# Transpositions in one pass, new orders of the work, and two experts' gates on GpSimd

## The reference, cut to what matters

```
# layer 0: attention, then a mixture of experts with one choice of experts for each image
q, k, v = 1x1 convolutions of LN_c(x)            # 8 query heads of 16, one key and value head
u0 = x + conv_out(softmax(q) @ (softmax(k) v^T))
logits = mean over tokens(LN_t(u0)) @ Wr          # one row of 8 for each image
top 2 of 8 experts: z = sum_w( gelu(u W1[e]) W2[e] )
t = u0 + LN_t(z + u) * gamma                      # u = LN_t(u0)
# layer 1: a 3x3 convolution with weights of sign(w), then experts chosen for each token
t = t + conv3x3(LN_c(t), sign(w) * mean|w|)
xn = LN_t(t);  p = softmax(xn @ gate_w);  g = p where p is one of the token's 2 largest, else 0
out = t + sum over all 8 experts of  g[:, e] * (gelu(xn W1[e]) W2[e])
```

## Time and profile before

| | |
|---|---|
| Median of the runs | 410.23 us (408.69, 410.23, 413.77) |
| The profiled execution's own time | 412.51 us |
| Its span, first to last instruction | 410.7 us |
| Mean granted clock of TensorE | 0.927 |
| TensorE matmuls busy | 344.7 us, 84% of the span |
| VectorE / ScalarE / GpSimd busy | 278.7 / 230.0 / 92.8 us |
| Start of expert 2's hidden matmuls, images 1 to 6 | 205.94, 235.85, 265.74, 295.64, 325.54, 355.44 us |

### The profile page before, as it was taken

One profiled execution on the slowest core, in us unless ns is written; L12 is line 12 of the kernel. 1 busy time (PEld: TensorE's weight loads), 2 busy tenths in 40 slices (PEclk: granted clock), 3 DMA queues, 4 the chain that ended last, 5 costly groups with the idle time before them and its releaser, 6 DMA issues.

```text
span 410.7 us, 5254 instructions
## 1 busy us (share of the span) xinstructions
PE 344.7 (84%) x1751; PEld 188.1 (46%) x1751; DVE 278.7 (68%) x587; ACT 230.0 (56%) x392; POOL 92.8 (23%) x77
## 2 busy tenths in 40 slices
...
GB/s 153 178 119 31 1 2 2 0 2 1 2 1 0 0 2 1 0 74 339 1 103 336 0 128 311 0 155 285 0 207 233 0 229 211 3 292 144 26 344 95
DMA packets 25835, 41.17 MB, mean 100 GB/s; under 512 B 15376, under 2 KB 16144, under 8 KB 25808
## 3 DMA queue, kind: packets, MB, share of 16 engines
...
...
## 4 chain that ended last, share of the span: by engine, by line
PE 41%; DVE 25%; issue 13%; ACT 10%; POOL 5%; DMA 3%; POOLq 1%; ACTq 0%; SPq 0%; DVEq 0%
PE ps L696 9%; PE ps L742 6%; PE ps L801 5%; POOL rstdA L457 4%; PE ps L605 3%; PE ps L712 3%; DVE HB L1186 3%; PE ps L618 2%; PE ps L530 2%; PE ps L513 2%; PE ps L727 2%; DVE qsum L964 2%; ACT XC L1336 2%; ACT HB L1388 2%; DVE ssA L1092 2%
## 5 line engine op out<-in xcount | busy, mean ns | idle before, releaser
L696 PE MATMUL ps<-ET,W1B 64*128 64x512 f32 x256 | 70.4, 655 | 6.9 <-ACT HB L1388 5.3
L1186 DVE TENSOR_TENSOR HB<-HB,GB 128x1024 f32<-128x1024 f32 x44 | 53.1, 1220 | 23.9 <-DMA GB<-spread 23.8
L1388 ACT ACTIVATE HB<-ps,B1B 128x1024 f32<-128x1024 f32 x44 | 47.8, 1111 | 9.4 <-PE ps L696 5.3
L457 POOL TENSOR_TENSOR rstdA<-varA,pow_half 128x8 f32<-128x8 f32 x16 | 28.8, 1801 | 90.8 <-DVE varA L886 90.8
L801 PE MATMUL ps<-HB,W2B 128*64 128x512 f32 x176 | 45.2, 617 | 3.7 <-DVE HB L1186 3.7
L457 POOL TENSOR_TENSOR rstdB<-varB,pow_half 128x8 f32<-128x8 f32 x8 | 14.0, 1750 | 124.7 <-DVE varB L886 124.7
L696 PEld LDWEIGHTS ps<-ET,W1B 64*128 64x128 f32 x256 | 21.9, 194 | 35.8 <-issue 12.0
L457 POOL TENSOR_TENSOR rstd<-var,pow_half 128x4 f32<-128x4 f32 (+1 forms) x24 | 29.0, 1217 | 21.1 <-DVE var L886 20.8
L742 PE MATMUL ps<-VP,WC 128*128 128x512 f32 x96 | 28.4, 450 | 1.4 <-ACT VP L1356 1.4
L1186 DVE TENSOR_TENSOR XC<-XC,GB 128x1024 f32<-128x1024 f32 x20 | 24.2, 1219 | 5.9 <-DMA GB<-spread 5.9
L472 POOL TENSOR_TENSOR QS<-QS,rqsum 128x512 f32<-128x512 f32 x16 | 16.9, 1057 | 44.1 <-DVE rqsum L967 44.1
...
## 6 DMA issues: line engine op xcount, KB each, us to landing
...
```

Of the source, the lines that this page charges most:

```text
L457: pool.tensor_tensor(out_, var, pow_half[:, 0:n], ALU.pow).then_inc(s[rstd_sem], 1)
L696: mm(ps[:, H_BANKS[n % 2][c], :], weights[half(c), :], tokens(half(c)), start=True, stop=True).then_inc(s["h"], 1)
L1186: tt(HG[b][e], HG[b][e], GB[:, e, :], ALU.mult).then_inc(s["f_hg"], 1)
L1388: av(HG[b][e], HID[n % 2], ACT.Gelu, bias=B1B[:, e:e + 1]).then_inc(s["gelu"], 1)
```

## The change

1. `residual` splits its 256-column matmul: the copy of x is now written by TensorE's transposition (`is_transpose=True`), the centred half stays a plain matmul with 128 columns. `u_to_channels` and the residual part of `f_start` become transpositions too.
2. `u_to_channels` no longer has the column of ones. ScalarE's copy into `UT` becomes two instructions with `accum_out`, which give the sums over tokens.
3. `f_start` now holds only the residual, and opens the accumulator before the outputs; the bias is a step of its own, `f_bias`.
4. GpSimd multiplies the hidden values of experts 4 and 7 with their gates, by the same kind of instruction as VectorE; each has its own semaphore, and SyncE's queue and `f_output` wait for the one that belongs to the expert.
5. All tables of orders are new. In the image tables the period begins at another step.

```diff
     return Steps(eng, sem, base)
 
 
+POOL_EXPERTS = (4, 7)
+
+
+def gated(b, e):
+
+    on_pool = e in POOL_EXPERTS
+    mine = [x for x in range(E) if (x in POOL_EXPERTS) == on_pool]
+    return "f_pg" if on_pool else "f_hg", len(mine) * b + mine.index(e) + 1
+
+
...
 PLAN = dict(
     pool=(
-        "b_rstd+1 a_rstd0+2 a_rstd1+2"
+        "f_gated4-1 a_rstd1+1 f_gated7-1 b_rstd+1 a_rstd0+2"
     ).split(),
...
+        "f_hidden6-1 f_hidden7-1 b_to_channels f_bias-1 b_gates f_start f_output2-1 f_hidden0 f_hidden1 "
         "f_output3-1 f_output4-1 f_hidden2 a_hidden0+2 b_gates_turned f_hidden3 f_hidden4 a_vT0+1 f_output5-1 "
...
     vec=(
-        "b_probs b_first a_ss1+1 b_second b_weights a_normalise+1 f_gated5-1 f_gated6-1 f_gated7-1 f_gated0 "
-        "b_residual+1 b_centre+1 f_gated1 b_ss+1 a_sum+2 f_gated2 a_ss0+2 b_normalise+1 f_gated3 a_zn+2 f_gated4 "
-        "b_logits+1 a_residual+2 a_centre+2"
+        "b_normalise f_gated3-1 a_zn+1 a_residual+1 b_logits a_centre+1 b_probs a_ss1+1 b_first b_second b_weights "
+        "a_normalise+1 f_gated5-1 f_gated6-1 f_gated0 f_gated1 b_residual+1 b_centre+1 f_gated2 b_ss+1 a_sum+2 "
+        "a_ss0+2"
...
 )
...
-        "rstd1_0 qnorm2-1 rstd1_1 rstd2_0-1 rstd2_1-1 qnorm3-1 qnorm0 qnorm1 rstd2_2-1 rstd2_3-1"
+        "qnorm3-2 rstd2_1-2 qnorm0-1 rstd2_2-2 qnorm1-1 rstd2_3-2 rstd1_0 rstd1_1 qnorm2-1 rstd2_0-1"
...
-        UT = sb("UT", [P, B, 4, P + 1])
+        UT = sb("UT", [P, B, 4, P])
+        USUM = sb("USUM", [P, B, 4])
...
                 for e in range(E):
-                    ge(sp, s["f_hg"], 8 * (b - 1) + e + 1)
+                    if b > 0:
+                        signal, count = gated(b - 1, e)
+                        sp.wait_ge(s[signal], count)
                     sp.dma_start(GB[:, e, :], spread[b, e:e + 1, :].broadcast_to([P, S])).then_inc(s[f"spread{e}"], 16)
...
+            def f_gated(e):
+                def part(b, par):
+                    pool.wait_ge(s["gelu"], TURN["f", e, b] + 1)
+                    pool.wait_ge(s[f"spread{e}"], 16 * (b + 1))
+                    pool.tensor_tensor(HG[b][e], HG[b][e], GB[:, e, :], ALU.mult).then_inc(s["f_pg"], 1)
+                return part
...
                         pe.wait_ge(s["u"], n - 1)
                     for j in range(UT_):
                         t = g + 4 * j
-                        ins = mm(a[:, j * 256:(j + 1) * 256], XC[:, p, t * P:(t + 1) * P], ic, start=(j == 0), stop=False,
+                        both = a[:, j * 256:(j + 1) * 256].rearrange("p (i x c) -> p i x c", i=2, x=2)
+                        mm(both[:, :, 0, :], XC[:, p, t * P:(t + 1) * P], ident, start=(j == 0), stop=False,
+                           is_transpose=True, skip_group_check=True)
+                        ins = mm(both[:, :, 1, :], XC[:, p, t * P:(t + 1) * P], cen, start=False, stop=False,
                                  skip_group_check=True)
...
                     for i in range(2):
-                        ins = mm(ps[:, UT_BANK, i * (P + 1):(i + 1) * (P + 1)],
-                                 U[:, 2 * p + i, UT_ * g:UT_ * g + UT_, :].rearrange("p h c -> p (h c)"), IDS[:, :],
-                                 start=True, stop=True)
+                        ins = pe.transpose(ps[:, UT_BANK, i * P:(i + 1) * P],
+                                           U[:, 2 * p + i, UT_ * g:UT_ * g + UT_, :].rearrange("p h c -> p (h c)"), ident)
...
             def f_start(b, par):
 
+                pe.wait_ge(s["b_t"], b + 1)
+                ge(pe, s["f_out"], b - 1)
                 for j in range(4):
-                    mm(acc(b)[:, j * P:(j + 1) * P], B2X[:, j, :], GT[:, par, :], start=False, stop=False,
-                       skip_group_check=True)
                     ins = mm(acc(b)[:, j * P:(j + 1) * P], TF[:, par, j].rearrange("p h c -> p (h c)"), ident,
-                             start=False, stop=False, skip_group_check=True)
+                             start=(j == 0), stop=False, is_transpose=True, skip_group_check=True)
                 ins.then_inc(s["f_start"], 1)
+
+            def f_bias(b, par):
+
+                pe.wait_ge(s["b_cwt"], b + 1)
+                for j in range(4):
+                    ins = mm(acc(b)[:, j * P:(j + 1) * P], B2X[:, j, :], GT[:, par, :], start=False, stop=False,
+                             skip_group_check=True)
+                ins.then_inc(s["f_bias"], 1)
...
             def f_output(e):
                 def part(b, par):
-                    if e == 0:
-                        ge(pe, s["f_out"], b - 1)
-                    pe.wait_ge(s["f_hg"], 8 * b + e + 1)
+                    signal, count = gated(b, e)
+                    pe.wait_ge(s[signal], count)
                     for c in range(2):
                         ins = mm(acc(b)[c * C:(c + 1) * C, :], W2B[:, e, :], HG[b][e][:, c * HALF:(c + 1) * HALF],
-                                 start=(e == 0), stop=(e == E - 1), skip_group_check=True)
+                                 start=False, stop=(e == E - 1), skip_group_check=True)
                     ins.then_inc(s["f_w2"], 1)
...
-            rd.done(vr(u8[:, :], UT[:, :, :, P], X, ALU.add))
+            rd.done(vr(u8[:, :], USUM[:, :, :], X, ALU.add))
...
-                [(f"f_gated{e}", f_gated(e)) for e in range(E)]
+                [(f"f_gated{e}", f_gated(e)) for e in range(E) if e not in POOL_EXPERTS]
...
-                    src = ps[:, UT_BANK, 0:2 * (P + 1)].rearrange("p (b n) -> p b n", b=2)
-                    av(UT[:, 2 * p:2 * p + 2, g, :], src, ACT.Copy).then_inc(s["uT"], 1)
+                    for i in range(2):
+                        ins = av(UT[:, 2 * p + i, g, :], ps[:, UT_BANK, i * P:(i + 1) * P], ACT.Identity,
+                                 accum_out=USUM[:, 2 * p + i, g:g + 1])
+                    ins.then_inc(s["uT"], 1)
```

More of the change, by code:

```diff
@@ L124 @@
-        "keys_values0+2 keys_values1+2 residual2+1 u_to_channels3 attend2+1 q_to_channels3+1 u_to_channels0+1 "
-        "queries0+2 residual3+1 queries1+2"
+        "queries2+1 kv_to_tokens+1 residual3 u_to_channels0 context+1 attend3 context_turned+1 q_to_channels0+1 "
+        "u_to_channels1 context_out+1 centre0+2 set_outputs+2 centre1+2 residual0+1 set_fold+2 queries3+1 "
+        "q_to_channels1+1 attend0+1 residual1+1 u_to_channels2 xn_to_channels0+2 attend1+1 xn_to_channels1+2 "
+        "keys_values0+2 keys_values1+2 q_to_channels2+1 set_second-2 queries0+2 queries1+2 residual2+1 "
@@ L132 @@
-        "normalise2_3-2"
+        "sum_squares2_0-2 set_bo-1 query_sum3-2 normalise2_0-2 key_max-1 query_max0-1 sum_squares2_1-2 "
+        "query_max1-1 normalise2_1-2 query_sum0-1 set_layer1-2 sum_squares2_2-2 order_rows1 key_norm-1 "
+        "pick_context-1 query_sum1-1 block_diagonal-1 sum_squares2_3-2 set_fold+2 normalise2_2-2 query_max2-1 "
+        "order_rows0+2 set_conv-1 sum_squares1_0 normalise2_3-2 sum_squares1_1 normalise1_0 query_sum2-1 "
+        "normalise1_1 query_max3-1"
     ).split(),
@@ L139 @@
+        "square1_1+2 query_channels0+1 query_exp2+1 set_fold+2 query_channels1+1 channels1_0+2 residual0+1 "
+        "channels1_1+2 query_exp3+1 keys_values0+2 keys_values1+2 residual1+1 query_channels2+1 u_channels2 "
+        "set_second-2 key_exp+2 u_channels3 query_exp0+2 query_channels3+1 residual2+1"
     ).split(),
@@ L373, in build @@
             "b_eT", "b_et", "b_gate", "b_lg", "b_exp", "b_top", "b_cwT", "b_cwt", "b_out",
-            "h", "gelu", "f_hg", "f_start", "f_w2", "f_out", "f_stored",
+            "h", "gelu", "f_hg", "f_pg", "f_start", "f_bias", "f_w2", "f_out", "f_stored",
         ) + tuple(f"spread{e}" for e in range(E))}
@@ L381, in build @@
         Q_BANK, QT_BANK, AT_BANK, UT_BANK = (2, 3), 4, (5, 6), 7
-        MEMSETS = 9
+        MEMSETS = 8
         A_BANK, B_BANK, ACC_BANK = 0, 1, (2, 7)
@@ L492, in b_rstd @@
                 rstd(varB[:, :], rstdB[:, :], TILES, b + 1, "b_var", "b_rstd")
+            def f_gated(e):
[4 more added lines that the diff above has]
+                return part
             periods(PLAN["pool"], dict(
-                [("a_rstd0", a_rstd(0)), ("a_rstd1", a_rstd(1)), ("b_rstd", b_rstd)]))
+                [("a_rstd0", a_rstd(0)), ("a_rstd1", a_rstd(1)), ("b_rstd", b_rstd)]
+                + [(f"f_gated{e}", f_gated(e)) for e in POOL_EXPERTS]))
         @block.tensor
@@ L701, in part @@
                     pe.wait_ge(s["a_sel"], 4 * b + 2 * k + 1)
-                    first_layer("a", k, b, W1S[:, k, :], lambda rows: UT[rows, b, :, 0:P])
+                    first_layer("a", k, b, W1S[:, k, :], lambda rows: UT[rows, b, :, :])
                 return part
```

33 lines of the change are left out of this document (10 added, 23 removed), and 5 rows, old and new, of the table pe.

## The result

The changed kernel takes **429.01 us** (median of four runs, 426.98 to 432.60), the kernel before 411.08 us beside it (four runs). The ratio is 1.044, with a 95% interval of 1.035 to 1.054: slower by 4.4%. The forecast was 420, with a range of 398 to 424: the sign of the likeliest case was right, the size too small. The profiled execution has a span of 427.3 us against 410.7, so +16.6, where the prediction's sum was +10.2.

The account below looks back on a forecast made before the run. TensorE was taken to bound both long stages, with VectorE not far behind. The terms -3.7 - 0.7 + 14.4 - 0.4 + 0.6 gave +10.2 us, 420.4 against the median, stated as 420; range 398 to 424.

Parts of the forecast that it names:

- The wait: Two-operand VectorE products behind GpSimd's gatings of experts 4 and 7: full 2.0 us wait each, adding 2.4 us a period.
- Rival A: Expert stage: no shutting out of VectorE worth the name, period 28.8 us, total 399.4 us, faster; chance 30%.
- Transpositions in the attention, -3.7: Attention units: two thirds of TensorE's saved 6.9 us come back, -4.4, and ScalarE's uncovered last unit costs +0.7.
- Image 0, -0.7: Logits' chain for image 0: gains 0.7 us from moving `a_residual` ahead of the logits.
- The product's length, 2.0: GpSimd's gating product over 1024 columns: 2.0 us, between bounds of 1.06 and 2.11.
- Six periods, +14.4: Expert stage, images 0 to 5: waits at expert 4's product (+0.87) and expert 7's (+1.5), 6 x 2.4 us.
- The last image, -0.4: Last image's period: no `a_zn` there, so only `f_start`'s saving on TensorE counts, -0.4 us.
- The end, +0.6: End of the run: three hidden steps instead of one after the wait, less 1.1 us of `f_start`; +0.6 after rounding.
- main case: Expert stage: both GpSimd products make VectorE wait fully; 420 us, own range 414 to 426, chance 47%.

Follow-up runs that it names:

- the memsets: Changed kernel with all gatings on VectorE and two unneeded 1024-column memsets at each of GpSimd's two product places: 400.40 us, ratio 0.977.
- experiment 11: Changed kernel with all gatings on VectorE, and layer 0's residual put back behind the gate logits: 397.51 us, ratio 0.966.

## Why the prediction fell short

- **The wait was right.** VectorE's products wait for nearly the whole of GpSimd's, at both places named, six times each. The Trainium skill (SBUF — State Buffer, "Who interferes with whom") describes this; the trace agrees with 2.84 us against 0.69, and the memsets, which read nothing, agree too. GpSimd's power of 8 columns reads SBUF as well, and no wait for it shows (below). The row that the prediction read it from, L925, holds as well: in the changed kernel (L951) one of its four instances still stands beside GpSimd's product and takes 1.10 us, the other three beside a power and take 0.22. Rival A's condition, no waiting, is what the kernel with all gatings on VectorE has: 397.9 us, against its 399.4. It had put the distance without products at 28.8; 29.3 was measured, and the front, 7.6 us shorter instead of 4.4, made up for it.
- **Transpositions in the attention, -3.7:** measured -6.9. What the prediction gave to the transpositions is what they bring in the old order (3.6). It put nothing down for the new orders of the units, which bring 1.7 alone and let another 1.6 of TensorE's saving come back. ScalarE's second copy and its accumulator reads (277 + 204 ns) were covered.
- **Image 0, -0.7:** measured -1.6 (8.5 less 6.9), but it is luck that the sign fits. With the residual put back (experiment 11) image 0's expert 2 starts at 166.14, without at 166.69. The start moves by up to 1.8 us between profiles of the same work, and the changed kernel's had a better clock: a mean of 0.70 from 120.3 to 165.8 us, against 0.65 in the same stretch of the kernel before (127.2 to 174.3).
- **The product's length, 2.0:** 2.35 us, the mean of L510. The estimate from the Trainium skill (GPSIMD Engine Reference, "Elementwise — side-by-side cycle accounting"), 2.25, was nearer; the row with 512 columns gave 2.11, which the prediction took for an upper bound and which was none. It is the smaller part of the error: VectorE's extra time is 2.15 and 2.19 us.
- **Six periods, +14.4:** measured +16.7, in steady state 4.1 us each instead of 2.4. With TensorE kept busy the distance is 32.28 = 29.9 + 2.4, the sum to a tenth, but by luck: from 28.8 to 32.3 the prediction gave the waits 3.5 us, and they take 3.0 on top of 29.28. What lacked is the granted clock: 1.75 us a period, since the stalls, from 0.70 to 2.24 us and from nothing to 1.28, are followed by work at half speed. It shows in four of the six distances (34.00, 34.04, 34.08 and 33.52 against 32.26), 6.6 us in all. That the part is only 2.3 us over the prediction is due to the first distance, 30.0 us, shorter than the 31.7 before. The prediction priced a stall as standing time alone: the clock is a term that it put at nothing without a reason.
- **The last image, -0.4. This is the step that failed.** "The last image's period has no `a_zn`: only f_start." It has no `a_rstd0` either, so expert 4's product follows `b_rstd`, and `b_normalise`, with TensorE behind it, meets it in place of `a_zn`. Measured +8.0, of which 5.7 go when this one meeting is taken away; the kernel then takes 422.6 us, inside the range. Of the 5.7, 3.8 are the clock again. So of what the prediction left out, the half clock costs about 10 us in the seven distances, and the last image's meetings 4.6 besides (8.4 less 3.8).
- **The end, +0.6:** measured +0.3, as a whole, but not by what was summed: with no product on GpSimd it is -1.2. Expert 4's product of image 7 makes one gating on VectorE last 2.18 us instead of 1.22 (at 415.05), a meeting that the prediction does not have. And `f_output0` behind `f_hidden5` gives back only 2.1 us of span over the whole run, and not at the end.

The errors partly cancel: -3.2 and -0.9 at the front, +2.3 in the periods, +8.4 in the last distance, -0.3 at the end: together 6.3 us over the sum of 10.2. The range ended at 424 since it was built from the main case's own terms; neither the clock nor the last period was in any case.
